# A transformer layer on one core: the last batch's second half weighs projected values, and the ending is put in another order

## What is computed

```python
q = jnp.einsum('btd,hdk->bhtk', x, wq)
k = jnp.einsum('btd,hdk->bhtk', x, wk)
v = jnp.einsum('btd,hdk->bhtk', x, wv)
...
s = jnp.einsum('bhik,bhjk->bhij', q, k)
s = s - 1e+30 * mask
p = jax.nn.softmax(s, axis=-1)
o = jnp.einsum('bhij,bhjv->bihv', p, v)
return jnp.einsum('bto,od->btd', o, wo)
...
x = _layernorm(x + attention(x), axis=-1)
x = _layernorm(x + ffn(x), axis=-1)      # ffn: gelu(x @ bw1.T + b1) @ bw2.T + b2, bw = mean|w| * sign(w)
```

## Time and profile before

| | |
|---|---|
| median of 3 runs | 279.47 us (278.9, 279.47, 280.8) |
| the profiled execution | 278.4 us |
| its span, first to last instruction | 276.6 us |
| TensorE busy | 260.7 us, 94% of the span |
| VectorE, ScalarE, GpSimd busy | 230.6, 224.7, 167.2 us |
| mean granted TensorE clock | 0.983 of 2.4 GHz |

### The profile page before, as it was taken

The page is one execution under the profiler, slowest core; times in us unless marked ns, Lnnn a source line. Parts: engine busy times, 40 slices in busy tenths (PEclk is TensorE's granted clock), DMA queues, the critical chain, the costliest instruction groups (busy, mean ns, idle before and its releaser), DMA issues.

```text
span 276.6 us, 5169 instructions
## 1 busy us (share of the span) xinstructions
PE 260.7 (94%) x1478; PEld 209.2 (76%) x1479; DVE 230.6 (83%) x638; ACT 224.7 (81%) x398; POOL 167.2 (60%) x258
## 2 busy tenths in 40 slices
PE   7799999999999999999999999999999999999960
PEld 3588889987688688868879688767885878897630
DVE  2889999999999996999989985999689738537884
ACT  3468964565897989996998999699999699999972
POOL 3033132613625598299912998477829987887772
PEclk9979999999999999999999999999999999999995
DMA  7943486479648936823675309724830720200323
GB/s 180 161 65 71 102 149 108 115 165 192 105 119 186 193 88 153 176 37 85 184 178 122 84 26 246 185 60 126 204 89 5 210 62 0 78 0 2 105 92 110
DMA packets 58012, 31.94 MB, mean 115 GB/s; under 512 B 33408, under 2 KB 54400, under 8 KB 57984
## 3 DMA queue, kind: packets, MB, share of 16 engines
q1 hardware_dynamic: 57024, 30.76, 49.6%
q10 hardware_dynamic: 960, 0.85, 1.2%
HBM read 9.18 MB, written 4.19 MB: 48 GB/s over the span
## 4 chain that ended last, share of the span: by engine, by line
PE 76%; DVE 8%; ACT 5%; DMA 5%; issue 4%; ACTq 1%; POOL 0%; SPq 0%; POOLq 0%; DVEq 0%
PE pair L589 17%; PE bank L606 17%; PE bank L632 5%; PE bank L674 5%; PE bank L620 4%; PE pair L650 4%; PE pair L651 4%; PE bank L682 3%; PE bank L683 3%; DMA out_dram<-res 2%; DMA sin_sb<-in_sin_dram 2%; PE bank L719 2%; PE pair L663 2%; PE bank L639 2%; PE pair L665 2%
## 5 line engine op out<-in xcount | busy, mean ns | idle before, releaser
L391 POOL TENSOR_TENSOR hid_lo<-hid,hid_hi 128x1024 fp32r<-128x1024 f32 x28 | 66.1, 2386 | 21.1 <-ACT hid_hi L1073 21.1
L1002 ACT ACTIVATE prob<-pair,negmax 128x128 f32<-128x128 f32 (+3 forms) x64 | 47.3, 742 | 17.0 <-DVE negmax L1455 15.4
L606 PE MATMUL bank<-probT,xa 128*128 128x512 f32 (+3 forms) x160 | 54.2, 482 | 0.3 <-DVE res L1565 0.3
L1455 DVE CUSTOM_DVE_ANT_0 pair<-pair,mask_row 128x128 f32<-128x128 f32 (+3 forms) x64 | 47.8, 760 | 6.7 <-PE pair L589 6.3
L606 PEld LDWEIGHTS bank<-probT,xa 128*128 128x128 f32 x160 | 29.1, 190 | 20.4 <-issue 15.8
L341 POOL TENSOR_TENSOR xT_lo<-xT,xT_hi 128x512 fp32r<-128x512 f32 x14 | 18.0, 1285 | 40.8 <-ACT xT_hi L1032 40.8
L1465 DVE STREAM_TRANSPOSE turned<-prob 128x128 f32<-128x128 f32 (+7 forms) x56 | 39.5, 723 | 0.5 <-ACT prob L1002 0.5
L589 PE MATMUL pair<-qkT_hi 128*128 128x512 f32 (+3 forms) x96 | 36.5, 380 | 1.4 <-ACT prob L1002 0.6
L589 PE MATMUL pair<-qkT_hi,qkT_lo 128*128 128x512 f32 (+3 forms) x96 | 33.1, 345 | 0.0
L589 PE MATMUL pair<-qkT_lo,qkT_hi 128*128 128x512 f32 (+3 forms) x96 | 33.1, 345 | 0.0
L1066 ACT ACTIVATE hid<-pair,b_sb,alpha 128x1024 f32<-128x1024 f32 x28 | 32.9, 1208 | 0.1
(11 more groups left out here) (116 smaller groups left out, 649.6 us busy)
## 6 DMA issues: line engine op xcount, KB each, us to landing
probT<-turned SPq DMA_DIRECT2D x96, 116.0 KB, 2.3
probT<-turned SPq DMA_DIRECT2D x128, 52.0 KB, 2.0
xq<-in_L_attn_x_dram SPq DMA_DIRECT2D x28, 128.0 KB, 3.9
xa<-in_L_attn_x_dram SPq DMA_DIRECT2D x7, 512.0 KB, 5.1
out_dram<-res SPq DMA_DIRECT2D x7, 512.0 KB, 3.4
hid<-in_L_ffn_w_dram SPq DMA_DIRECT2D x2, 256.0 KB, 3.1
out_dram<-res SPq DMA_DIRECT2D x2, 256.0 KB, 2.3
xa<-in_L_attn_x_dram SPq DMA_DIRECT2D x1, 256.0 KB, 3.6
```

Of the source, the lines that this page charges most:

```text
L391: pool.tensor_tensor(hid_lo[:, j, :], hid[:, j, :], hid_hi[:, j, :].bitcast(F32), ALU.subtract).then_inc(s_hid_lo[j], 1)
L606: ins = pe.matmul(bank_of["px", g, c][:, 0:n * P], xa[c % 2][:, j, :], probT[g][:, :, TG * j:TG * j + n, :].rearrange("p n m i -> p m n i" ...
L1002: act.activation(prob[r % 3][:, 0:(r + 1) * P], pair_of["score", r, c][:, slice(*columns(r))], ACT.Exp, scale=-1.0, bias=negmax[:, r:r + 1 ...
L1455: dve.tensor_tensor_reduce(mine, mine, mask_row[:, T - (r + 1) * P:T], -1.0, -MASKED, ALU.add, ALU.min, negmax[:, r:r + 1]).then_inc(s_max ...
```

## The change

Three things, all in the last 60 us of the program.

1. Rows 4 to 7 of batch 7 are weighed in the other order. `project_values(h, 7)` makes x wv wo from `xT` (already there for queries and keys) for both halves, and ScalarE's `values_copy` brings it to SBUF, into `xq`, which is no longer needed. `weigh_values(r, 7)` then multiplies the turned probabilities with it and writes the attention's result as it stands, by rows, so that `pxT_copy(1, 7)` and `project_out(1, 7)` go. Row copies of batch 7 write whole 128-column tiles (`tilesT`, the same memory as `probT[1]`).
2. `hidden_high_half(h, j)` waits for `s_down[h]` and not for `s_down[1]`. `hidden_low(2, 6)` is done by VectorE and not by GpSimd.
3. The last batch's steps are put in another order on TensorE, ScalarE and VectorE, and both `fill` calls go, nine matmuls.

```diff
+            def project_values(h, c):
+
+                pe.wait_ge(s_xT[h], c + 1)
+                dst = next_bank("values", h, c)
+                for t in range(TG):
+                    me = slice((TG * h + t) * P, (TG * h + t + 1) * P)
+                    ins = pe.matmul(dst[:, t * D:(t + 1) * D], xT[:, me], wvo[:, :], start=True, stop=True)
+                ins.then_inc(s_values_pe[h], 1)
+
+            def weigh_values(r, c):
+
+                g, spot = SPOT[r]
+                if r == TG:
+                    pe.wait_ge(s_values[0], 1)
+                    pe.wait_ge(s_values[1], 1)
+                    next_bank("attn", g, c)
...
+                mine = bank_of["attn", g, c][:, (r % TG) * D:(r % TG + 1) * D]
+                for j in range(r + 1):
+                    ins = pe.matmul(mine, tilesT[:, TG * j + spot, :], values[:, j, :], start=j == 0, stop=j == r)
...
             up(1, B - 3)
+            project_values(0, B - 1)
             down(0, B - 4)
             down(1, B - 4)
...
             turn_y(1, B - 4)
+            project_values(1, B - 1)
             weigh_group(0, 0, 3, B - 1)
...
             turn_x1(0, B - 1)
-            project_out(1, B - 1)
             up_half(0, 0, B - 1)
             up_half(0, 1, B - 1)
             down(0, B - 2)
+            turn_x1(1, B - 1)
             down(1, B - 2)
-            turn_x1(1, B - 1)
-            fill(7)
+            up_half(1, 0, B - 1)
             turn_y(0, B - 2)
             turn_y(1, B - 2)
-            fill(2)
-            up_half(1, 0, B - 1)
             up_half(1, 1, B - 1)
...
+            def values_copy(h, c):
+                act.wait_ge(s_values_pe[h], 1)
+                act.activation(values[:, TG * h:TG * (h + 1), :].rearrange("p n d -> p (n d)"), bank_of["values", h, c][:, :],
+                               ACT.Copy).then_inc(s_values[h], 1)
...
             gelu(0, B - 3)
+            values_copy(0, B - 1)
             y_half(0, B - 4)
...
             gelu(3, B - 3)
+            values_copy(1, B - 1)
             hidden_high(1, B - 3)
             pxT_copy(0, B - 1)
```

More of the change, by code:

```diff
@@ L115, in attention_ffn_kernel @@
         ln2 = sb("ln2", [P, LN_STEPS, NT])
+        values = xq[:, :].rearrange("p (n d) -> p n d", d=D)
+        tilesT = probT[1][:, :, :, :].rearrange("p a n b -> p (a n b)").rearrange("p (n c) -> p n c", c=P)
         magnitude = hid[:, 0, 0:2 * H].rearrange("p (w h) -> p w h", w=2)
@@ L467, in _ @@
             hidden_low(1, B - 2)
-            hidden_low(2, B - 2)
             hidden_low(3, B - 2)
@@ L515, in wait_freed @@
                     pe.wait_ge(s_pxT[i], c + 1)
+                if task == "values":
+                    pe.wait_ge(s_values[i], 1)
                 if task == "attn":
@@ L555, in setup_wvo @@
                 pe.matmul(bank_of["wvo", 0, 0][:, P:P + D], wvT, wo_sb, start=True, stop=True).then_inc(s_prep_pe, 1)
[L557 to L561, removed]
             def setup_turn_sgn1():
@@ L955, in _ @@
             turn_y(1, B - 3)
[L956 to L959, removed]
+            weigh_values(4, B - 1)
+            weigh_values(5, B - 1)
+            weigh_values(6, B - 1)
+            weigh_values(7, B - 1)
             turn_x1(0, B - 1)
-            project_out(1, B - 1)
             up_half(0, 0, B - 1)
@@ L1385, in _ @@
             hidden_high(3, B - 2)
-            pxT_copy(1, B - 1)
             x1T_high(0, B - 1)
@@ L1393, in _ @@
             gelu_half(0, 0, B - 1)
-            second_norm(6, B - 4)
             gelu_half(0, 1, B - 1)
@@ L1397, in _ @@
             gelu_half(0, 3, B - 1)
-            second_norm(7, B - 4)
+            second_norm(6, B - 4)
             y_half(0, B - 2)
@@ L1401, in _ @@
             x1T_high(1, B - 1)
+            hidden_high_half(0, 2, B - 1)
             y_half(1, B - 2)
-            hidden_high_half(0, 2, B - 1)
+            second_norm(7, B - 4)
+            gelu_half(1, 0, B - 1)
             hidden_high_half(0, 3, B - 1)
+            gelu_half(1, 1, B - 1)
             second_norm(0, B - 3)
@@ L1507, in row_copy @@
                     dve.wait_ge(s_px[NT - 1], c)
+                src = pair_of["rowT", r, c][:, BANK:(r + 1) * P]
+                if c == LAST:
+                    dve.tensor_copy(tilesT[:, squares(r, TG, r), :],
+                                    src.rearrange("p (m q) -> p m q", q=P)).then_inc(s_rowT_dve, 1)
+                    return
                 dve.tensor_copy(probT[g][:, :, squares(r, TG, r), :].rearrange("p n m j -> p m n j"),
@@ L1510, in row_copy, with hidden_low @@
                                 ).then_inc(s_rowT_dve, 1)
+            def hidden_low(j, c):
+                dve.wait_ge(s_hid_hi[j], c + 1)
+                dve.wait_ge(s_down[NG - 1], c)
+                dve.tensor_tensor(hid_lo[:, j, :], hid[:, j, :], hid_hi[:, j, :].bitcast(F32),
+                                  ALU.subtract).then_inc(s_hid_lo[j], 1)
             def hidden_high_half(h, j, c):
                 dve.wait_ge(s_gelu[j], c + 1 + h)
-                dve.wait_ge(s_down[NG - 1], c)
+                dve.wait_ge(s_down[h], c)
                 dve.tensor_copy(hid_hi[:, j, half(h)], pair_of["up_half", 2 * h + j // 2, c][:, half(j % 2)]
@@ L2052, in _ @@
             statistics2(0, B - 3)
+            hidden_low(2, B - 2)
             x1T_low(0, B - 1)
```

16 lines of the change are left out of this document (12 added, 4 removed).

## The result

The changed kernel takes 283.54 us (median of 4 runs, 282.99 to 284.65), the kernel before 279.19 us in the runs beside it (278.42 to 280.8): 1.0187 times the time before, with a 95% interval of 1.0132 to 1.0241. The forecast was 284.4 us in a range of 280.2 to 287.4, and slower. The profiled execution took 283.01 us, its span is 281.2.

A forecast was written before the change was run, and what follows sets the result against it. TensorE (94% of the span) and ScalarE were taken as full, then from 248.6 us batch 7's ring through ScalarE, VectorE and GpSimd. 1.9 + 2.5 + 0.6 = +5.0 us gave 284.4 us, range 280.2 to 287.4.

The forecast's parts named there:

- Part A: Values matmuls and their copies on full TensorE and ScalarE make up(0, 6) start later: +1.9 us.
- Part B: project_out(1, 7) and pxT_copy(1, 7) removed: almost nothing at up_half(0, 0), then up_half(1, 0) 1.9 us earlier.
- Part D: Reordered ending: second_norm(7, 4) behind y_half(1, 6) delays GpSimd's factors and ScalarE's norms, +2.5 us.
- Part C: hidden_low(2, 6) moved to VectorE, ending before x1T_low(0) can start: 0, bounds 0 and +2.3 us.
- Part E: Nine fills removed: TensorE idles after down_quarter(1, 0) and its clock may fall, +0.6 us.
- Rival 1: Part B's early start reaches the end, Part A may be only 1.1: 278.7 us, not slower; chance 0.09.
- Rival 2: Only Part A counts, Part D's queue costs just what Part B won: 281.4 us; chance 0.16.
- Rival 3: GpSimd gets the shared port before VectorE, x1T_low(0) comes 2.3 us late: 286.7 us; chance 0.08.
- rival 4: A double-counted wait is covered and the removed matmuls count in full: 275.9 us, faster; chance 0.07.

The follow-up runs named there:

- e3: The kernel before with the values alone added, order, waits and fills kept: tail (last exponential to end) 59.00 us against 57.09, median 280.79 us, 1.0054 of before.
- e2: The changed kernel with the values taken out, pxT_copy(1, 7), project_out(1, 7) and weigh_row put back: tail 61.41 us against 62.95, median 283.48 us, 1.0139 of before.
- f3: e4 with GpSimd scaling all eight batch 5 rows, ScalarE's y_half(·, 7) and VectorE's low parts moved earlier: median 279.00 us, 0.9958 of before, tail 57.19.
- e1: The changed kernel with second_norm(7, 4) moved back ahead of y_half(0, 6) on ScalarE: tail 59.61 us against 62.95, median 281.88 us, 1.0096 of before.
- e4: The changed kernel with both the values taken out and second_norm(7, 4) moved back: tail 58.80 us, median 280.52 us, 1.0073 of before.
- g5: e1 with TensorE's order around batch 6's down passes as before, without fills: tail 61.65 us against 59.61, median 283.66 us, 1.0107 of before.
- f2: The changed kernel with hidden_low(2, 6) back on GpSimd: tail 62.55 us against 62.95.
- f6: The changed kernel with a third residual buffer, so residual2(0, 6) need not wait for batch 4's store: tail 63.26 us against 62.95.
- f1: The changed kernel with zero matmuls in TensorE's idle time and turn_y(1, 6) put behind up_half(1, 1): tail 62.04 us against 62.95.
- g4: The kernel before without its two fill calls (nine matmuls): tail 56.95 us against 57.09.
- g2: e4 with the zero matmuls of f1: tail 60.37 us against 58.80.
- g3: The changed kernel with f6's third buffer and f1's zero matmuls together: tail 63.21 us against 62.95.

## Why the prediction was right, point by point

**Part A, +1.9: right, and shown alone** by e3, +1.91. Its path came out as worked (229.52 for 229.5, 236.27 for 236.25): two copies through a full ScalarE, and the bank rotation that moved by one. Taken out of the finished change (e2) the same part is worth 1.54. Of the 0.37 less, 0.10 is the clock's wait, longer there (1.01 for 0.91), and 0.23 goes at residual1(4): against the anchor x1T_low(0) starts 1.86 us earlier in e2 (30.40 for 32.26), but residual1(4) only 1.63 (31.24 for 32.87), since it waits for project_out again. Part B had 0.28 for this.

**Part B.** project_out and the pxT copy brought nothing at their place: up_half(0, 0) waits 1.42 us for x1T_low(0), forecast 1.4. up_half(1, 0) starts at 258.52 + 1.26 - 1.91 = 257.87 on before's scale, forecast 257.8 and before 259.67. So the 1.8 us are there, and no run shows them at the end (f3 has them too, among other changes). What I had not said is why it would not pay even without the queue of part D: what ends last is batch 6's second half (y_half(1, 6), residual2, statistics2, second_factors(6), its norms on ScalarE, y_half(1, 7)), not batch 7's up pass. To turn batch 7's x1 first, TensorE lets down(1, 6) wait (0.73 above), and y_half(1, 6) is 0.7 us late in e1: 40.69 against 38.09 + 1.91. There is a second holder, in ScalarE's order. second_factors(6) waited for VectorE's statistics before; in e1, as in e4 and g5, it waits for ScalarE's norms of batch 5. Before, e1 and g5:

```profile
262.17 0.21 POOL L323 TENSOR_TENSOR ln<-stat 128x8 f32<-128x8 f32 x1 [1.05 <-DVE stat L1574]
263.55 0.21 POOL L329 TENSOR_TENSOR ln<-stat 128x8 f32<-128x8 f32 x1 [1.81 <-ACT res L1129]
265.57 0.21 POOL L329 TENSOR_TENSOR ln<-stat 128x8 f32<-128x8 f32 x1 [4.04 <-ACT res L1129]
```

Two gelus of half 1 now stand ahead of those norms, which start 2.75 us behind y_half(1, 6) in e1 (261.73 - 258.98) and started 1.68 behind it before (259.28 - 257.60). All this is read from the traces. g5, meant to show the first holder, did not, for its clock fell, and no run moves the gelus back: how the two share what is left stays open.

**Part C, 0: right** (f2). The added add on VectorE started at 248.06 and took 1.79 us. GpSimd's hidden_low(0) and (1) ended at 244.02 + 4.74 = 248.76; the 1.09 us from there to 249.85 are what the add needs by itself, if it waited for them like the one of the earlier trace rows. GpSimd's next, hidden_low(3), took 3.02, where its four took 9.42 in all before, 2.4 each:

```profile
244.02 4.74 POOL L397 TENSOR_TENSOR hid_lo<-hid,hid_hi 128x1024 fp32r<-128x1024 f32 x2 [0.97 <-ACT hid_hi L1102]
249.05 3.02 POOL L397 TENSOR_TENSOR hid_lo<-hid,hid_hi 128x1024 fp32r<-128x1024 f32 x1 [0.29 <-ACT hid_hi L1102]
```

VectorE got in ahead of hidden_low(3), as forecast: GpSimd stood 0.29 us without input between the two. On before's scale the add ends at 249.20, forecast near 249.2. GpSimd lost some 0.6 us, which nothing waits for. The Trainium skill (SBUF — State Buffer, section "SBUF: two separate sides") says that the first in holds the shared port pair and the other blocks; these rows agree with that.

**Part D, +2.5: the mechanism right, the size 0.5 short.** With before's scale and without the values (a shift of 1.26 - 1.91 = -0.65) the chain reads, measured and forecast:

| | measured | forecast |
|---|---|---|
| y_half(1, 6) starts | 257.91 | 257.88 |
| second_norm(7, 4) starts | 258.59 | 258.60 |
| second_factors(5) starts | 259.23 | 259.26 |
| ScalarE's wait ahead of batch 5's norms | 1.89 | 2.1 |
| GpSimd's norms of batch 5 end | 264.74 | 264.76 |
| second_factors(6) starts | 265.36 | 264.86 |

The step that failed is the last: "second_factors(6), as long as the other, about 0.1 + 3.65". I let it follow GpSimd's norms at once. It waited 0.61 for statistics2(1, 6), because residual2(0, 6) stood 4.57 us for the store of batch 4. f6 shows this: without that wait second_factors(6) had none either, and started 0.59 us earlier against the anchor (47.17 for 47.76). That store is the DMA that the moved norm issues, and I had followed the norm's semaphore to GpSimd but not its DMA to the buffer's next writer. e1 takes away all three holders at once (GpSimd's start, VectorE's and TensorE's waits) and the slow clock behind them, and wins 3.34. 0.91 of it is the clock's by f1, which leaves 2.43 for the queue and the store. The 0.61 that is left of part D (59.61 - 57.09 - 1.91) falls to the rest of the order, by the two holders under part B; no run shows it by itself.

**Part E, +0.6: direction right, 0.91 measured** (f1). But the step's heading was wrong: it blamed the removed fills. In before's order they are worth nothing (g4, -0.14), and in the changed one they would have stood elsewhere than the idle time that let the clock fall. I had TensorE idle once, behind down_quarter(1, 0); it waited 2.26 us ahead of down_quarter(0, 0), for the bank that the store held, and 0.94 behind (1, 0). That time came from part D, and e1 without fills kept its clock. The low clock is hardly a chance of this one trace: the mean granted clock was 0.970 to 0.977 in the changed kernel's four executions, 0.979 to 0.994 in 25 of before. In g5 the clock fell behind a wait where before had fills; no run tries g5 with them. The Trainium skill (TensorE: Matmul & The Clock Gate, Part 1) says that an idle array falls to half rate until it has been busy; the falls come behind its waits, which agrees (in e4 behind 1.22 and 0.46 us), but neither the rule nor the waits in my rows tell e1 from e4.

**Sum.** The tail grew by 5.86: 1.91 (A), 0.91 (clock), and 3.04 for the order, where 1.9 + 0.6 + 2.5 = 5.0 was forecast. The median grew by 4.35 only: 1.26 of the difference lies at 172 us, where the change has no part, and the rest (0.25) in how the profiled executions stand to their medians. So the sum was 0.9 too low for the stretch that was edited, and the trace of before happened to have a wait there that the one of after had not; 284.4 came within 0.9 of 283.54 partly by luck.

**Rivals.** Rival 1 fell with the 5.09 us wait, and e1 shows that it falls even without the queue. Rival 2 has the time of e3, not of the change. Rival 3 is out by the order of the two adds, rival 4 by the sum.

## What to carry to other kernels

When an instruction is put behind another in a full queue, follow everything that it sets free: the engine that takes its result, the DMA that stores it, and whoever writes that buffer next. Here 0.5 us of work, moved past one wait, cost 3.3 us of the tail by three such followers. An earlier start counts only on the chain that ends last, so first find which batch's half that is, on every engine that it goes through, and do not let it wait for the others.

## What the runs showed of the hardware

- **TensorE's last waits do not tell whether the clock falls.** Behind waits of TensorE of 1.22 and 0.46 us it stayed at 1.00 in e1 and fell to 0.50 in e4; behind 1.11 and 0.46 it stayed in g2, behind 1.12 and 0.47 it fell in g3; behind one of 1.56 it stayed in g4, behind 1.94 it fell in g5. Once down it stayed there for some 3.5 us in g5 and e4, and for 7 us in the changed kernel. Between the ten executions of e1 the mean granted clock went from 0.977 to 0.992. A difference of 1 us between two single traces can be this alone.
- **A store's landing is a wait of its own.** 512 KB took 3.2 us from issue to landing (the median of seven), and one wait for such a store near 172 us, 2.04 us in one trace and none in the other, goes with a shift of 1.3 at the anchor.
- **Zero matmuls are free only in true idle time.** In f1 ten of them ran while VectorE waited for the store, and the tail grew shorter by 0.91; in g2 VectorE waited 2.85 us for the transposes behind them, and the tail grew by 1.57.
